# An attention kernel's operand preparation: one copy-and-split pair moved four rounds earlier, a queue wait taken out, and two small schedules shifted

## The chip, the cores and the metric

The kernel runs on one core of one Trainium2 chip. The metric is the device time of one execution in microseconds (us), lower is better. The engines are named PE (TensorE, matrix multiply), DVE (VectorE), ACT (ScalarE), POOL (GpSimd) and SP (SyncE, which here only issues DMAs). PEld is PE's loading of weights.

## What the reference computes

Inputs are x and a context of 4 x 1024 x 512, two gates, and three weight matrices. The first half is a layer norm of x, then attention of 16 heads (32 wide) with the context as keys and values, rotary embedding and a linear bias, and no projections; the second half a feed-forward block with rounded weights and activations.

```python
x = x + tanh(g_xattn[0]) * xattn(layernorm(x), ctx, ctx, 16)
x = x + tanh(g_ffn[0]) * ffn(layernorm(x), w_gate, w_up, w_down)
# xattn: q, k = rope(q), rope(k); softmax(q k^T / sqrt(32) + slope * (j - i)) v
# ffn:   quantized( silu-like(x w_gate^T) * (x w_up^T) ) w_down^T
```

## The kernel before, in words

**Rounds and groups.** Attention goes over 16 groups `p`. A group is one batch and four heads, 128 columns wide. Each group has two halves of queries, and each half eight blocks of keys, so a group has 16 rounds, `w` = 0 to 15 in the code; I call them round 0 to round 15 of group p. A round does on PE four score products (L888), four products for row maxima of the queries three rounds and one half-group ahead (L876), and the product of the previous round's exponentials with the values (L925). ACT takes four exponentials (L1091), of 128 x 512 each. DVE takes two maxima (L1290), of 128 x 1024 each, one for each pair of L876 products. PE's order inside a round is written out by hand: score, score, maximum, maximum, maximum, score, maximum, score, then the values product, then in some rounds a sum of the denominators (L953), a turn of the output (L935) or a turn of a weight tile (L894).

**Two wide banks.** The maxima products land in two PSUM banks of 1024 columns that are used in turn. The order of all uses is a list, and each use waits until the use two places before it has been read out (`bank_release`). The output turns, the weight turns and the "part" uses below stand in the same list. Scores have two banks of their own: score n waits for exponential n - 2.

**Preparing the next groups.** For a later group the queries are normalized by ACT in eight pieces (L1044, `NORM_TILES` tells in which rounds), rotated by POOL in fp32 (`rope`), and split in a high and a low fp16 part in the buffer `S`, in two halves of four blocks. A half takes three steps. ACT writes the high part (`high_part`, L1069). ACT copies the fp32 value to a wide bank (`copy_part`, L1075). DVE subtracts the high part from that copy and writes the low part (`low_part`, L1309). `Step.high` and `Step.low` say in which round each half is split: the query's two halves in rounds 0 and 2 (high) and 1 and 6 (low), the key's in rounds 9 and 12 (high) and 10 and 14 (low). ACT does its high part, then its copy, at the end of a round, after the four exponentials, and DVE does its low part after the round's two maxima. In round 3 or 4 of a group POOL starts a DMA that adds one sum of exponentials onto another (L1822, `Ps<-P`), and again in rounds 6, 11 and 14 or so; the sums go into L953.

**The transposes.** SP sends each half of `S` through a transposing DMA into `QA` or `KA` (`load_stack`, L626). `Step.stack` places these in rounds 0 and 1 (keys), 2 and 9 (queries). SP does not count rounds: it issues in order, each as soon as its waits have been met. The query's second half waits in addition for the accumulation that POOL starts in round 6. The queries' second half is first read in round 13.

**Weights.** The gate weights are prepared beside attention by a table of steps (`gate_weight_jobs`, a step is a round counted over all groups, 16 to a group). At step 85 DVE forms scales (`wscale_r`). At step 89 `wall` brings a maximum to all partitions by DVE instructions alone: one reduction, four transposes and four reductions (L1364 to L1370). `wnorm_1` to `wnorm_3` are three small operations after it.

Of the kernel before, what the change touches and what calls it, by code (L numbers as in the profile page):

```python
# [51 lines left out]
def gate_weight_jobs():  # L52

    jobs = {}

    def put(g, *job):
        jobs.setdefault(g, []).append(job)

    for k in range(OT):
        put(32 + 4 * k, "wload", 0, k)  # L60
        put(38 + 4 * k, "wmax", 0, k)
    put(83, "wscale", 0)
    put(85, "wscale_r", 0)
    put(89, "wall", 0)
    put(94, "wnorm_1", 0)
    put(96, "wnorm_2", 0)
    put(98, "wnorm_3", 0)
    for k in range(OT):
        put(90 + 8 * k, "wload", 0, 12 + k)
        put(100 + 8 * k, "wdivide", 0, k)  # L70
        put(106 + 8 * k, "wround", 0, k)
        put(108 + 8 * k, "wrounded", 0, k)
        put(110 + 8 * k, "wscaled", 0, k)
        put(115 + 8 * k, "wturn", 0, k)
        put(118 + 8 * k, "wstore", 0, k)
    return jobs
# [23 lines left out]

NORM_TILES = {1: (0,), 4: (1, 2, 3), 5: (4,), 6: (5, 6), 7: (7,)}


class Step:


    def __init__(self, g):
        self.g = g  # L110
        self.hf, self.s = hf, s = g // 8, g % 8
        self.p, self.qc = p, qc = hf // 2, hf % 2
        w = 8 * qc + s
        self.inside = 0 <= hf < NHALF
        m = g + 8 + LEAD
        self.hm, self.im = m // 8, m % 8
        self.maxima = 0 <= self.hm < NHALF

        self.out = hf - 1 if s == (3 if hf == NHALF else 4) and 1 <= hf <= NHALF else None


        self.high = self.low = self.key_bias = None
        if -1 <= p and p + 2 < NQ:
            if w == 8:
                self.key_bias = p + 2
            elif w in (9, 12):
                self.high = (p + 2, 1, w // 12)
            elif w in (10, 14):
                self.low = (p + 2, 1, w // 14)
        if 0 <= p and p + 1 < NQ:  # L130
            if w in (0, 2):
                self.high = (p + 1, 0, w // 2)
            if w in (1, 6):
                self.low = (p + 1, 0, w // 6)
        self.side = []

        self.rope = None
        if 0 <= p and p + 2 < NQ and w in (0, 2, 6, 8, 10, 14):
            k = (0, 2, 6, 8, 10, 14).index(w)
            self.rope = (p + 2, 1 - k // 3, k % 3)  # L140
        elif -10 <= g <= -5:
            self.rope = (1, 1 - (g + 10) // 3, (g + 10) % 3)
        self.add = hf - 1 if s == 5 and 1 <= hf < NHALF else None
        self.norm = []
        if 2 <= p + 2 < NQ:
            self.norm += [(p + 2, i) for i in NORM_TILES.get(w, ())]
        if g < -7:
            self.norm += [(1, 2 * (g + 11)), (1, 2 * (g + 11) + 1)] if g < -8 else [(1, 6), (1, 7)]
        self.norm.sort()

        self.load_context = p + 3 if w == 1 and 0 <= p and p + 3 < NQ else None
        self.load_columns = p + 3 if w == 6 and 0 <= p and p + 3 < NQ else None

        self.stack = {0: (1, 0), 1: (1, 1), 2: (0, 0), 9: (0, 1)}.get(w) if 0 <= p and p + 1 < NQ else None
        self.rows = self.hm if 0 <= self.hm < NHALF and self.im == 7 else None
        self.store = p - 1 if w == 7 and 1 <= p <= NQ else None


        last, inside = hf == NHALF - 1, self.inside and hf < NHALF - 1
        self.sum = (hf, s // 2) if last and s % 2 == 1 else (hf, {1: 0, 4: 2, 7: 1}[s]) if inside and s % 3 == 1 else None  # L160
        self.accumulate = (hf, s // 6, s - 1) if inside and s in (3, 6) else None
        self.dens = None
        if s == 6 and inside:
            self.dens = (hf, 0)
        elif s in (1, 2) and 1 <= hf < NHALF:
            self.dens = (hf - 1, s)
        elif last and s in (3, 5, 7):
            self.dens = (hf, s // 2 - 1)
        elif hf == NHALF and s == 1:
            self.dens = (hf - 1, 3)  # L170
        self.num_out = hf - 1 if s == 1 and 1 <= hf <= NHALF else None
        self.den_out = hf - 1 if s == (2 if hf == NHALF else 3) and 1 <= hf <= NHALF else None

        self.stats = None
        if w >= 14 and 0 <= p < NQ:
            self.stats = (p, 0, w - 14)
        elif w == 0 and 1 <= p <= NQ:
            self.stats = (p - 1, 0, 2)
        elif p == NQ and 5 <= w < 8:
            self.stats = (p - 1, 1, w - 5)  # L180
        elif 6 <= w < 9 and 1 <= p < NQ:
            self.stats = (p - 1, 1, w - 6)
        self.aggregate = self.deviation = None
        self.ffn_loads = (hf, s) == (NHALF - 1, 6)


def all_steps():
    steps = [Step(g) for g in range(-8 - LEAD, 8 * NHALF + 8)]
    for jobs in (layer_norm_jobs(), gate_weight_jobs()):
        for st in steps:  # L190
            st.side += jobs.get(st.g, [])
    for i, st in enumerate(steps):
        if 8 * st.qc + st.s == 8 and 1 <= st.p <= NQ and st.p % 4 == 0:
            if st.p < NQ:
                steps[i + 1].aggregate = st.p // 4 - 1
                steps[i + 4].deviation = st.p // 4 - 1
    return steps
# [30 lines left out]
def part_no(p, w, half):  # L228

    return 4 * p + 2 * (1 - w) + half + 1  # L230
# [7 lines left out]
def score_no(hf, kt, h):  # L238
    return 32 * hf + 4 * kt + h + 1
# [352 lines left out]
def sync_program(e, K):  # L592
# [19 lines left out]
    def load_stack(p, w, half):  # L612
        if p >= 2:
            e.wait_ge(K.pe_score, score_no(2 * (p - 2) + 1, 7, 3))
        if w:
            e.wait_ge(K.a_kb, p + 1)
        if p == 0 and half == 0:
            e.wait_ge(K.v_aux, 2)
        if p > 0 and (w, half) == (0, 1):

            e.wait_ge(K.d_acc[1], 16 * (2 * p - 2) + 16)
        e.wait_ge(K.a_hi, part_no(p, w, half))
        e.wait_ge(K.v_lo, part_no(p, w, half))
        rows = slice(4 * half, 4 * half + 4)
        dst = (K.QA, K.KA)[w][p % 2][:, rows, :, :].rearrange("c i h t -> c (i h) t")
        e.dma_start_transpose(dst, K.S[w][:, rows, :, :, :].rearrange("t i h n d -> t (i h n d)")).then_inc(K.d_st[w][half], 16)  # L626
# [63 lines left out]
    for w, half in ((1, 0), (1, 1), (0, 0), (0, 1)):  # L690
        load_stack(0, w, half)
# [3 lines left out]
    for st in STEPS:  # L695
        if st.load_context is not None:
            load_context(st.load_context)
        if st.stack is not None:
            load_stack(st.p + 1, *st.stack)
# [4 lines left out]
        if st.store is not None:  # L704
            p = st.store
# [1207 lines left out]
```

## Time and profile before

| | |
|---|---|
| median of 3 runs | 1842.67 us (1841.62 to 1842.9) |
| the profiled execution's own time | 1842.9 us |
| span in its trace | 1840.9 us |
| PE busy | 1651.6 us, 90% |
| DVE busy | 1486.9 us, 81% |
| ACT busy | 1240.9 us, 67% |
| POOL busy | 814.5 us, 44% |
| mean granted TensorE clock | 0.967 |

The span is from the first to the last instruction; the execution's own time holds about 2 us more. Busy time of PE is a union of records that overlap, so a busy PE is not PE at its peak. Times in views are microseconds from the start of the span, unless they are marked ns. Attention runs from about 62 to 953 us.

### The profile page before, as it was taken

What the parts mean: (1) busy time and instruction counts of PE and PEld (TensorE: products, weight loads), DVE (VectorE), ACT (ScalarE), POOL (GpSimd) and SP (SyncE); (2) the same over time, 40 slices, a digit from 0 to 9 for tenths busy, and PEclk for the clock granted to TensorE, in tenths of its full rate; (3) what the DMA queues carried; (4) which work ended last, traced back from release to release, by engine and by line L of the source; (5) the groups of instructions that cost most, each with busy time, mean ns of one, the idle gap of its engine ahead of it and who ended that gap; (6) DMA issues with size and microseconds to landing.
All of it is one profiled execution on the core that took longest, in us unless ns stands there. A gap on an engine that the chain in (4) does not pass through costs nothing. (4 is left out here: it accounts for less than half of the span.)

```text
span 1840.9 us, 24655 instructions
## 1 busy us (share of the span) xinstructions
PE 1651.6 (90%) x8679; PEld 603.5 (33%) x8679; DVE 1486.9 (81%) x2125; ACT 1240.9 (67%) x1972; POOL 814.5 (44%) x457
## 2 busy tenths in 40 slices
PE   2899999999999999999969999999999910599999
PEld 0222322222322323322213444444444400244444
DVE  6899889998888888888746998868889998855551
ACT  3577888888888888887642332339896699854440
POOL 6489988989999998996620010200000000000000
PEclk9999999999999999999998999999999965799999
DMA  6586878677678786766446898759983469864541
GB/s 170 138 184 156 173 167 181 143 153 156 148 162 170 146 171 142 151 132 138 81 160 168 269 258 254 225 162 277 285 263 134 132 233 285 262 204 167 167 168 66
DMA packets 334202, 331.46 MB, mean 180 GB/s; under 512 B 204640, under 2 KB 263392, under 8 KB 325888
## 3 DMA queue, kind: packets, MB, share of 16 engines
q1 hardware_dynamic: 325152, 264.89, 51.8%
q0 software_dynamic: 8928, 65.02, 17.7%
q8 instruction: 68, 1.11, 0.2%
q14 instruction: 54, 0.44, 0.1%
HBM read 139.92 MB, written 76.55 MB: 118 GB/s over the span
## 5 line engine op out<-in xcount | busy, mean ns | idle before, releaser
L1091 ACT ACTIVATE P<-quad 128x512 f32<-128x512 f32 x1024 | 556.5, 598 | 152.5 <-PE quad L888 149.9
L1290 DVE TENSOR_REDUCE cm<-quad 128x1 f16<-128x1024 f32 x512 | 601.2, 1216 | 71.6 <-PE quad L876 69.2
L1843 POOL TENSOR_TENSOR Ps<-P,P 128x2048 f32<-128x2048 f32 x93 | 424.4, 4564 | 106.3 <-ACT P L1091 106.3
L876 PE MATMUL quad<-KA,QA 100*128 100x512 f16 x1024 | 326.5, 392 | 43.6 <-DMA QA<-S 22.8
L888 PE MATMUL quad<-QA,KA 101*128 101x512 f16 x1024 | 353.7, 386 | 6.7 <-ACT P L1091 5.5
L925 PE MATMUL quad<-P,cg 128*32 128x512 f32 x2048 | 273.6, 606 | 5.2 <-ACT numT L1125 5.2
L968 PE MATMUL quad<-x_hl,Wu 128*128 128x512 f16 x1152 | 249.0, 379 | 2.4 <-DMA Wu<-wt_scratch 2.4
L968 PE MATMUL quad<-x_hl,Wg 128*128 128x512 f16 x1152 | 249.3, 379 | 1.7 <-DMA x_hl<-xs 1.7
L1013 PE MATMUL quad<-Wd,oh 128*128 128x512 f16 x768 | 228.6, 379 | 0.0
L888 PEld LDWEIGHTS quad<-QA,KA 101*128 101x128 f16 x1024 | 83.5, 97 | 331.9 <-ACT P L1091 242.5
L1175 ACT ACTIVATE ev<-quad 128x1024 f32<-128x1024 f32 x96 | 97.2, 1013 | 124.3 <-PE quad L968 118.3
L876 PEld LDWEIGHTS quad<-KA,QA 100*128 100x128 f16 x1024 | 98.6, 99 | 181.9 <-DVE cm L1290 59.1
L968 PEld LDWEIGHTS quad<-x_hl,Wu 128*128 128x128 f16 x1152 | 112.6, 98 | 138.5 <-DMA Wu<-wt_scratch 2.8
L968 PEld LDWEIGHTS quad<-x_hl,Wg 128*128 128x128 f16 x1152 | 112.5, 98 | 138.3 <-issue 3.1
L1551 DVE TENSOR_REDUCE mxt<-ev 128x1 f32<-128x1024 f32 x96 | 116.5, 1214 | 41.5 <-ACT ev L1175 41.2
L1013 PE MATMUL quad<-Wd,ol 128*128 128x512 f16 x384 | 145.5, 379 | 0.0
L1810 POOL TENSOR_TENSOR wq<-wl,wsc 128x512 f32<-128x512 f32 x36 | 41.1, 1141 | 218.3 <-DVE wl L1423 218.3
L1200 ACT ACTIVATE sgm<-gq,qs 128x1024 f32<-128x1024 int16 x96 | 110.1, 1147 | 39.0 <-DVE sgq L1593 37.4
L1689 DVE SCALAR_TENSOR_TENSOR xr<-quad,qs,xr 128x512 f32<-128x512 f32 x32 | 23.9, 750 | 114.6 <-PE quad L1013 110.1
L1013 PEld LDWEIGHTS quad<-Wd,oh 128*128 128x128 f16 x768 | 75.1, 98 | 90.6
L974 PE MATMUL quad<-ident,column 128*128 128x128 f32 x3 | 1.4, 456 | 112.8 <-DVE column L1359 112.8
L953 PE MATMUL quad<-Ps,ones 128*32 128x512 f32 x776 | 101.0, 592 | 1.1 <-POOL Ps L1843 0.8
(163 smaller groups left out, 1945.9 us busy)
## 6 DMA issues: line engine op xcount, KB each, us to landing
Ps<-P POOLq DMA_DIRECT2D x62, 1024.0 KB, 7.6
gate_scratch<-ev SPq DMA_DIRECT2D x48, 512.0 KB, 3.8
gt<-gate_scratch SPq DMA_DIRECT2D x48, 512.0 KB, 5.7
up_scratch<-ev SPq DMA_DIRECT2D x48, 512.0 KB, 3.4
uf<-up_scratch SPq DMA_DIRECT2D x48, 512.0 KB, 4.9
uf<-up_scratch SPq DMA_DIRECT2D x96, 256.0 KB, 3.6
wt_scratch<-wh SPq DMA_DIRECT2D x72, 128.0 KB, 2.3
cg<-in_ctx_dram SPq DMA_DIRECT2D x16, 512.0 KB, 4.7
```

The source lines that it names most:

```text
L876: mm = e.matmul(K.bank(use, c), K.QA[p % 2][0:100, 4 * qc + qt, h, :], K.KA[p % 2][0:100, 4 * c:4 * c + 4, h, :], start=True, stop=True)
L888: e.matmul(K.score[h % 2], K.KA[p % 2][0:101, kt, h, :], K.QA[p % 2][0:101, 4 * qc:4 * qc + 4, h, :], start=True, stop=True).then_inc(K.pe ...
L925: mm = e.matmul(K.num[32 * h:32 * h + 32, :], K.cg[(p + 1) % 4][:, kt, 32 * h:32 * h + 32], K.Pb[before.g % NP][:, h, :], start=kt == 0, s ...
L953: mm = e.matmul(K.den[32 * h:32 * h + 32, :], K.ones[:, :], K.Ps[n % 2 if hf == NHALF - 1 else n][:, h, :], start=n == 0, stop=n == (3 if ...
L968: mm = e.matmul(K.quad[z][:, 512 * h:512 * h + 512], W(part, c), K.x_hl[:, x, c0:c0 + 512], start=n == 0, stop=n == 11)
L1013: mm = e.matmul(ps, o[k][:, ot, sl], K.Wd[r][:, ot, :], start=ot == m == 0, stop=ot == OT - 1 and m == 2)
L1091: e.activation(K.Pb[pb][:, h, :], K.score[h % 2], ACT.Exp, scale=SCALE / (QPOW * KPOW)).then_inc(K.a_exp, 1)
L1175: e.activation(K.ev[k % NEV][:, :], K.quad[k % 4][:, :], ACT.Copy).then_inc(K.a_ev, 1)
L1200: e.activation(K.sgm[n % NSG][:, :], view(n), ACT.Sigmoid, scale=sg).then_inc(K.a_sig, 1)
L1290: e.tensor_reduce(cm[:, col:col + 1], K.quad[UNIT["max", hm, u] % 2][:, :], AX.X, ALU.max).then_inc(K.v_max, 1)
L1551: e.tensor_reduce(K.mxt[:, col:col + 1], K.ev[k % NEV][:, :], AX.X, ALU.max, apply_absolute_value=True).then_inc(K.v_mx, 1)
L1843: e.tensor_tensor(K.Ps[n][:, :, :], K.Pb[(st.g - 1) % NP][:, :, :], K.Pb[st.g % NP][:, :, :], ALU.add).then_inc(K.g_sum, 1)
```

## The change

Four edits. The low part of the second half of the queries goes from round 6 to round 2, behind the high part of the same half. The wait of its transposing DMA on the accumulation is taken out. Tile 0 of the normalization leaves round 1, and the tiles behind it move up by one place: three tiles in rounds 4 and 6, one in 5 and 7. In the weight table `wall` goes two steps earlier (89 to 87) and the three small operations behind it five.

```diff
-    put(89, "wall", 0)
-    put(94, "wnorm_1", 0)
-    put(96, "wnorm_2", 0)
-    put(98, "wnorm_3", 0)
+    put(87, "wall", 0)
+    put(89, "wnorm_1", 0)
+    put(91, "wnorm_2", 0)
+    put(93, "wnorm_3", 0)
...
-NORM_TILES = {1: (0,), 4: (1, 2, 3), 5: (4,), 6: (5, 6), 7: (7,)}
+NORM_TILES = {4: (0, 1, 2), 5: (3,), 6: (4, 5, 6), 7: (7,)}
...
-            if w in (1, 6):
-                self.low = (p + 1, 0, w // 6)
+            if w in (1, 2):
+                self.low = (p + 1, 0, w - 1)
...
-        if p > 0 and (w, half) == (0, 1):
-
-            e.wait_ge(K.d_acc[1], 16 * (2 * p - 2) + 16)
```

## Rows read from the trace of the kernel before

**Rows 1.** The page's first line.

```profile
span 1840.9 us, 24655 instructions
```

**Rows 2.** Windows, groups 1 and 10: length, busy PE, PEld, DVE, ACT, POOL, clock, DMA.

```profile
119.00:177.40 58.40, 54.95 (x321) 15.55 (x321) 57.14 (x88) 45.81 (x86) 53.37 (x41) 1.00 0.75 170
621.30:677.80 56.50, 54.89 (x330) 16.72 (x328) 48.35 (x63) 48.46 (x91) 51.41 (x25) 1.00 0.75 159
```

**Rows 3.** PE in order of time, group 10, start of round 3: start, length, what, count.

```profile
632.10 0.81 PE L876 MATMUL quad<-KA,QA 100*128 100x512 f16 x3
632.75 0.38 PE L888 MATMUL quad<-QA,KA 101*128 101x512 f16 x1
```

**Rows 4.** ACT in order of time, group 10, end of round 2 and start of round 3.

```profile
630.40 1.05 ACT L1069 ACTIVATE S<-t 128x1024 f16<-128x1024 f32 x1
631.35 0.62 ACT L1149 ACTIVATE wi<-wl 128x512 int16<-128x512 f32 x1
632.08 1.08 ACT L1091 ACTIVATE P<-quad 128x512 f32<-128x512 f32 x2
```

**Rows 5.** Group 10: copy and low part of round 1; DVE's next but one pair.

```profile
626.82 0.65 ACT L1075 ACTIVATE quad<-t 128x512 f32<-128x512 f32 x1
...
627.60 0.69 DVE L1309 SCALAR_TENSOR_TENSOR S<-quad,S 128x512 f16<-128x512 f32 x1 [0.37 <-ACT quad L1075]
...
632.73 2.36 DVE L1290 TENSOR_REDUCE cm<-quad 128x1 f16<-128x1024 f32 x2 [1.39 <-PE quad L876]
```

**Rows 6.** Group 10, round 4: DVE reads out a turned weight tile, PE takes the bank.

```profile
635.86 0.69 DVE L1414 TENSOR_TENSOR wh<-quad,wh 128x512 f16<-128x512 f32 x1 [0.77 <-ACT wh L1100]
...
636.61 0.39 PE L876 MATMUL quad<-KA,QA 100*128 100x512 f16 x1 [0.55 <-DVE wh L1414]
```

**Rows 7.** PE in order of time, group 10, round 6.

```profile
642.83 1.06 PE L876 MATMUL quad<-KA,QA 100*128 100x512 f16 x3
```

**Rows 8.** PE in order of time, group 3, round 8.

```profile
260.07 0.96 PE L876 MATMUL quad<-KA,QA 100*128 100x512 f16 x3
```

**Rows 9.** Group 0, end of round 2 and start of round 3: ACT, then PE.

```profile
73.78 1.06 ACT L1069 ACTIVATE S<-t 128x1024 f16<-128x1024 f32 x1
...
74.58 0.81 PE L876 MATMUL quad<-KA,QA 100*128 100x512 f16 x3
75.38 0.39 PE L888 MATMUL quad<-QA,KA 101*128 101x512 f16 x1
```

**Rows 10.** DVE in order of time, group 5, rounds 6 to 10.

```profile
367.08 0.68 DVE L1309 SCALAR_TENSOR_TENSOR S<-quad,S 128x512 f16<-128x512 f32 x1
367.68 0.86 DVE L1497 BATCH_NORM_STATS2 st<-x2s 128x6 f32<-128x128 f32 x4
368.45 2.34 DVE L1290 TENSOR_REDUCE cm<-quad 128x1 f16<-128x1024 f32 x2
...
376.42 0.18 DVE L1364 TENSOR_REDUCE spread<-wmx 128x32 f32<-128x32 f32 x1
...
378.79 2.36 DVE L1290 TENSOR_REDUCE cm<-quad 128x1 f16<-128x1024 f32 x2
```

**Rows 11.** PE, group 5: a score of round 9, the first of round 10, maxima of round 11.

```profile
373.93 0.38 PE L888 MATMUL quad<-QA,KA 101*128 101x512 f16 x1
...
376.82 0.60 PE L888 MATMUL quad<-QA,KA 101*128 101x512 f16 x2
...
381.20 0.98 PE L876 MATMUL quad<-KA,QA 100*128 100x512 f16 x3
```

**Rows 12.** Group 10: POOL's accumulation, SP's transpose, PE's denominators; then L626 over the span.

```profile
644.11 0.89 POOL L1822 DMA_DIRECT2D Ps<-P  x1
...
654.14 2.29 SPq L626 DMA_TRANSPOSE QA<-S  x1
...
658.86 1.04 PE L953 MATMUL quad<-Ps,ones 128*32 128x512 f32 x8
...
DMA to landing us min/median/max: 4.2/5.0/11.6
```

## The prediction

> **What bounds the kernel now.** I first set the span [rows 1] against the execution's own time: the sum below is made against 1842.9 us. The windows by group come next. In group 10 PE is busy 54.89 of 56.50 us, DVE 48.35, ACT 48.46; in group 1 DVE is busy 57.14 of 58.40 [rows 2]. So over most of attention PE sets the pace. In group 1, where the layer norm's statistics still run beside it, DVE does. All four edits lie in attention, and what follows it only starts later or earlier.
>
> Then I read rounds on all engines in order of time. The reader is to see that PE has nearly no slack and that a delay of PE is not made good. Three maxima products come 0.22 us apart, so that three of them last 0.81, the last being 0.38 long, and the third score stands 0.65 behind the first of them [rows 3]. That score also waits for the round's first exponential, which starts at 632.08 and is some 0.6 long, half of the 1.08 of two plus the overlap [rows 4]: it ends at about 632.68, and the score starts at 632.75. So both legs, PE's own queue and scores over exponentials, are tight at once; whatever holds one product inside PE's queue lengthens the round by about as much.
>
> The third maxima product of a round is the sensitive one. It opens the second bank. It waits for the use two places before in the list, which is the second maximum of the round before, or, when a part stands between, that part's DVE read. In group 10's round 6 three products last 1.06 instead of 0.81 [rows 7]: held 0.25 by the maximum. In round 4 the same product waits for a weight tile's read that starts at 635.86 and is 0.69 long, and starts at 636.61, 0.06 behind its end [rows 6]. These are the prices that I use.
>
> **Edit 1, the low part from round 6 to round 2.** Nothing is added or removed: per group one ACT copy (0.65 or 0.61 long) and one DVE subtraction (0.69). It is done for groups 0 to 14, 15 times. What it removes: in the bank list of round 7 the third product now waits for round 6's second maximum, not for the part. The hold of round 6 itself does not go, since it comes ahead of the part and is made by DVE's queue in rounds 4 and 5 (read-out of the output, transposes). In groups 2 to 4, where DVE has a weight maximum of 0.68 in round 6 too, a backlog reaches round 8: three products last 0.96 in place of 0.81 [rows 8], held 0.13 or so. With a DVE operation of 0.6 out of rounds 6 and 7 that goes: 3 x 0.12 = 0.4 gained. From group 6 on there is no such hold to win.
>
> What it adds: the copy now stands behind the high part of the same round. In group 10's round 2 the high part starts at 630.40 and the next ACT operation at 631.35 [rows 4]; that is the place the copy takes, since the code puts it ahead of side work. It ends 0.61 later, at 631.96. DVE started its low part in round 1 at 627.60, 0.13 behind the copy's end at 627.47 [rows 5]; here that gives 632.09, and an end at 632.78 with 0.69. DVE is idle at that time, 1.39 us before its next maximum [rows 5], so its queue does not delay it. PE follows 0.06 later, as in rows 6, at 632.84. The product that waits is the third of round 3, which now starts at 632.10 + 0.43 = 632.53 [rows 3]. Held: 0.31. The last score of the round has a few hundredths of slack, so I take 0.28 for the round. In rounds with side work on ACT the first exponential comes late too (the operation of 0.62 moves back by half a microsecond, of which 0.11 is idle now: 631.97 to 632.08 [rows 4]), about 0.3 to 0.4, and by the same amount beside the first, not on top. The bounds of this term: nothing, if the copy were done by ACT ahead of the high part, which the code excludes, so 0.2 from the scatter of the three handovers; above, 0.4 from ACT's leg.
>
> The same for groups 2 to 14: 13 x 0.28 = 3.6 us. Group 0's round 2 has no denominators on PE, so less room: the high part starts at 73.78, the next ACT operation at 74.73, the copy there would end at 75.34, the low part run from 75.47 to 76.16, and the third product start at 76.22 in place of 74.58 + 0.43 = 75.01. The third score then starts at 76.44 in place of 75.38 [rows 9]: 1.06 us. I take off 0.1 for group 0's own backlog in round 8: 0.95. In group 1 DVE has 1.26 us of idle in all [rows 2]; the operation that goes out of round 6 comes in in round 2, ahead of all of its later waits: 0, between -0.6 and +0.6.
>
> **Edit 2, the weight maximum in round 7 of group 5, in place of round 9.** It is a row of nine DVE operations, from 376.42 until the next maximum at 378.79: 2.37 us [rows 10]. DVE works without a pause there since round 5 has the scale operations too. Rounds 7 and 8 are short ones, without denominators; rounds 9 and 10 are long, and DVE catches up in them, which is why the maximum costs little now: a hold of 0.17 of the three products in round 11 (0.98 long) and a late start of about 0.2 [rows 11], 0.33 together. After the change: DVE's low part is out (367.08 to 367.68, 0.60), so round 7's pair starts at 367.85 in place of 368.45. The pair takes 2.26 (2.34 less an overlap of 0.08), the nine operations run from 370.11 to 372.48, a reduction takes 0.6, and round 8's pair starts at 373.08; its second maximum starts 1.13 later and ends at 375.43. Round 9's third product waits for that: 375.49, and the score behind it at 375.71, in place of 373.93 [rows 11]. From that score to the first of round 10 it is 2.89 now (376.82 less 373.93), of which some 0.24 is a wait for ACT that the delay covers. So 375.71 + 2.65 = 378.36 in place of 376.82: 1.54 later; less 0.33 for round 11, 1.2 us. This holds the first edit's gain in group 5. Bounds: 0, if DVE's row went into idle time, to 2.4, its whole length. The three small operations behind it move into rounds 9, 11 and 13: below 0.1.
>
> **Edit 3, normalization tiles.** Round 1 loses an ACT operation behind which ACT is idle, round 4 keeps three, round 6 gets a third where the copy went. Round 7's stays, so that POOL's rotation in round 8 is not earlier. Zero; it is hidden in ACT's idle time.
>
> **Edit 4, the wait of the transposing DMA.** SP issues it at 654.14, when the accumulation issued at 644.11 has landed [rows 12]: 10.0 us. Without the wait it goes behind the store of the same group, some seven us earlier. Nothing waits for it before round 13, so nothing is gained. What is queued behind it on SP (a weight tile, the row of round 12) is not waited for either. What it may cost is the accumulation itself: PE needs it at 658.86, 14.75 behind its issue [rows 12], so 4.7 us of slack. A transpose lands in 5.0 at the median [rows 12]. If its whole time were added to the accumulation's 10.0, it would land 0.3 late. So zero, up to 0.3 for each of 14 groups.
>
> A page of the Trainium skill speaks on this, and against the change: "DMA: Bandwidth & Descriptors", section "Queues, rings and completion order", says that each DMA engine goes round between its queues packet by packet. By that rule POOL's accumulation and SP's transpose share the engines while both are in flight, and the landing would move back. By rule the sum would be up to 4 us higher than mine; the rows of this trace, where the two are kept apart in round 6, don't show it.
>
> **Sum.** 0.95 + 3.6 - 0.4 + 1.2 = 5.4, of which I round off to 5.3: 1842.9 + 5.3 = 1848.2 us. The median of the runs shown is 0.2 under the profiled execution, so against it the forecast is 1848.0.
>
> **Rivals.**
> (a) The copy is not what PE waits for, or the delay is made good. Speaks for it: 0.3 us is three handovers of 0.06 to 0.13, each of which I carry over from another round. Against it: both legs are tight in rows 3 and 4. Then 0.95 and 1.2 at most remain, less 0.4: 1843 to 1845, no change to be told. It decides at a low part that ends by 632.47.
> (b) The transpose collides with the accumulation, and the denominators' product of round 10 waits. Price: at a transpose of 5.0 us 0.3 per group, 14 groups: +4, so 1852. With the longest, 11.6 [rows 12], 6.9 per group, about +95; I give that no weight. Against it: the store and weight transfers ahead of the transpose on SP's queue keep it back anyway. It decides at a landing more than 14.7 us after the issue.
> (c) Faster: if the hold in rows 7 is made by the copy and the part in round 6 after all, the change takes 0.25 from each of 15 groups, 0.4 from rows 8 and group 5's part, and round 3 hides the copy: -3.8 to -4.5, 1838.7. It decides where DVE's pair in round 6 starts. Against it: the part comes after the held product.
> (d) Edit 4 does nothing, since SP is held otherwise at that time: no change to the sum.
>
> **Chances.** Forecast 0.62; (b) 0.08, also slower; (a) 0.22; (c) 0.08. What a measurement of this kernel tells from no change is about 0.2%, 3.7 us: below 1839.0 it is faster, above 1846.4 slower. The forecast's own range reaches from 13 x 0.2 and half of edit 2 (+3.5) to 13 x 0.4 and all of it (+8.5), so a part of it, 0.05, lies within 0.2%. Slower 0.65, the same 0.27, faster 0.08. The range takes in most of (a), not (c): 1843.0 to 1852.0.
>
> **What would show it.** Right: in rounds 3 of groups 2 to 14 the three maxima products last about 1.1 us and not 0.81, with a wait for L1309; group 5 has PE wait for DVE in round 9 by well over 1 us; groups 6 to 14 are each 0.28 longer; L626 is issued before the accumulation lands, and L953 does not wait for it. Wrong: no wait in round 3; a wait of L953 for the accumulation in round 10 (b); three products in round 6 at 0.81 (c). The prediction fails most easily by the 0.28, which counts 13 times.

## The result, and the profile after

The changed kernel takes 1865.22 us in the median of four runs (1858.28 to 1875.63), the kernel before 1842.14 (1841.43 to 1842.9, four runs); the ratio is 1.013, with a 95% interval of 1.0082 to 1.0179. The forecast was 1848.2 us with a range up to 1852.0: the direction was right, the size was not.

The profiled execution of the changed kernel took 1867.81 us. Its page begins with the first line below, against [rows 1]; the second is from the page's groups (busy, mean ns of one, idle before it and what ended that idle time), and tells where to look: PE idled 17.6 us for `Ps` ahead of the denominators, which are L950 here. All later lines of the code stand three lower than in the trace of before.

```profile
span 1865.9 us, 24641 instructions
...
L950 PE MATMUL quad<-Ps,ones 128*32 128x512 f32 x776 | 102.3, 599 | 18.7 <-DMA Ps<-P 17.6
```

To find the place, take the time from one round's first exponential to the next round's as the length of the round. From the first exponential to the end of the last it is 914.87 us, and 891.07 before: 23.8 of the 25.0 us of span lie in attention. By group: 19.61 in group 1, 3.08 in group 5, 0.15 to 0.31 in each of groups 2 to 4 and 6 to 14 (3.1 together), none in 15, and -2.02 in group 0. Group 1 has 18.87 of it in round 10, 22.61 us long in place of 3.74, and 0.83 in round 11.

**Group 1.** These are SP, POOL and PE in order of time (start, length, then the instruction, with idle time and its releaser in brackets).

```profile
142.84 1.78 SPq L609 DMA_DIRECT2D xl<-in_x_dram  x1
144.77 8.30 SPq L623 DMA_TRANSPOSE QA<-S  x1
...
140.85 0.20 POOL L1742 TENSOR_TENSOR nwt<-mv,eps 128x8 f32<-128x8 f32 x1
...
144.84 0.20 POOL L1742 TENSOR_TENSOR nm<-nwt,minus 128x8 f32<-128x8 f32 x1
145.32 0.92 POOL L1819 DMA_DIRECT2D Ps<-P  x1 [0.28 <-ACT P L1088]
...
156.55 1.06 PE L922 MATMUL quad<-P,cg 128*32 128x512 f32 x8
175.19 1.94 PE L950 MATMUL quad<-Ps,ones 128*32 128x512 f32 x8 [17.57 <-DMA Ps<-P]
```

The reader is to see the order. POOL does ten small operations of the layer norm from 140.85 to 145.04, and only then issues the accumulation, at 145.32. SP, which no longer waits for it, has issued the transpose at 144.77, 0.55 ahead. The accumulation lands at 175.15, 29.8 us after its issue, and PE starts 0.04 later. Three loads and a store that SP issued from 140.91 to 142.84 stand ahead of the transpose; all four are still in flight at 145.32, and the last lands at 150.3. In all other groups the accumulation is issued first, and there it hardly suffers: in groups 2 to 14 it lands 8.5 to 11.1 us after its issue (7.8 to 10.8 before), and it is the transpose that takes longer, 9.7 to 14.0 (4.3 to 6.0 before). This is group 10, where nothing is late (compare [rows 12]):

```profile
666.76 0.89 POOL L1819 DMA_DIRECT2D Ps<-P  x1
...
670.41 8.08 SPq L623 DMA_TRANSPOSE QA<-S  x1
...
681.51 1.04 PE L950 MATMUL quad<-Ps,ones 128*32 128x512 f32 x8
```

and the shortest, median and longest landing times of L623 and, behind it, of L1819 over the span:

```profile
DMA to landing us min/median/max: 4.3/5.9/28.5
...
DMA to landing us min/median/max: 6.9/7.5/29.8
```

The view of the DMA queues shows that both transfers slow down together (a packet is a piece of a transfer that one of the 16 DMA engines carries). It is that of 146 to 175 us after, in which POOL's next accumulation, issued at 162.04, has begun too (q0 is POOL's queue, q1 SP's; the share is that of 16 engines' time):

```profile
DMA packets 3207, 2.73 MB, mean 94 GB/s; under 512 B 2139, under 2 KB 2877, under 8 KB 3020
...
q0 software_dynamic: 208, 1.52, 67.3%
q1 hardware_dynamic: 2998, 1.20, 50.5%
```

and the same for 147 to 161 us of the kernel before, which holds its accumulation and its transpose:

```profile
DMA packets 3316, 2.34 MB, mean 167 GB/s; under 512 B 2134, under 2 KB 3044, under 8 KB 3187
...
q1 hardware_dynamic: 3171, 1.28, 36.7%
q0 software_dynamic: 144, 1.05, 36.1%
```

A packet of POOL's took 0.673 x 16 x 29 / 208 = 1.50 us, against 0.361 x 16 x 14 / 144 = 0.56; one of SP's 78 ns against 26, by the same working. These are means, and the single packets in the trace tell more. The median packet lasts as long as before, 0.63 us on POOL's queue and 18 ns on SP's. But 34 of POOL's 208 last over 0.7 us, up to 13.8, and hold 69% of the queue's packet time, where before none of 144 did; on SP's queue 172 of 2998 last over 0.12 us and hold 70%, where before none did. At each full microsecond of the stall 14 to 28 packets are in flight. So the engines were not idle, but for most of the time they sat on a few very long packets, and moved 94 GB/s in place of 167.

Behind the stall PE is slow too: its clock falls at 162.3, after PE has waited since 157.6. The windows (length, busy PE, PEld, DVE, ACT, POOL, granted clock, DMA) show the clock near the lower of its two levels, 1.2 GHz, until 179.5; the eight denominator products at 175.19 last 1.94 and not 1.04. That is the rest of the 18.9 us, and the 0.83 of round 11.

```profile
157.00:175.00 18.00, 0.62 (x8) 0.00 (x0) 2.86 (x5) 0.86 (x2) 6.21 (x4) 0.65 0.91 79
175.00:179.50 4.50, 4.31 (x15) 1.12 (x16) 0.52 (x1) 1.57 (x3) 0.00 (x0) 0.52 0.61 127
```

**Group 10** is as forecast. ACT, DVE and PE around the start of round 3, against [rows 3 to 5]:

```profile
652.75 1.05 ACT L1066 ACTIVATE S<-t 128x1024 f16<-128x1024 f32 x1
653.70 0.60 ACT L1072 ACTIVATE quad<-t 128x512 f32<-128x512 f32 x1
654.22 0.62 ACT L1146 ACTIVATE wi<-wl 128x512 int16<-128x512 f32 x1
...
654.43 0.69 DVE L1306 SCALAR_TENSOR_TENSOR S<-quad,S 128x512 f16<-128x512 f32 x1 [0.73 <-ACT quad L1072]
...
654.45 1.12 PE L873 MATMUL quad<-KA,QA 100*128 100x512 f16 x3
655.40 0.38 PE L885 MATMUL quad<-QA,KA 101*128 101x512 f16 x1
```

The window of the whole group, against [rows 2]:

```profile
643.70:700.50 56.80, 55.05 (x330) 16.74 (x329) 48.41 (x63) 48.35 (x92) 51.41 (x25) 1.00 0.75 158
```

The copy stands behind the high part, the low part ends at 655.12, and PE's third product comes after it: three products last 1.12, not 0.81. The third score is 0.95 behind the first product, not 0.65.

**Group 5.** PE in order of time, and then the window of the same stretch.

```profile
390.60 0.60 PE L885 MATMUL quad<-QA,KA 101*128 101x512 f16 x2
392.73 0.60 PE L873 MATMUL quad<-KA,QA 100*128 100x512 f16 x2 [1.53 <-DVE cm L1287]
393.86 0.39 PE L873 MATMUL quad<-KA,QA 100*128 100x512 f16 x1 [0.53 <-DVE cm L1287]
...
395.24 1.94 PE L922 MATMUL quad<-P,cg 128*32 128x512 f32 x8
396.94 1.45 PE L950 MATMUL quad<-Ps,ones 128*32 128x512 f32 x8
```

```profile
392.90:397.00 4.10, 3.57 (x18) 0.77 (x20) 3.76 (x4) 2.23 (x4) 2.32 (x2) 0.68 0.52 121
```

PE waits for DVE twice, and right behind that eight products of the output last 1.94, where they lasted 1.06 before the wait (L922 in group 1, above), at a mean granted clock of 0.68.

**Group 0.** PE's hold is there: the third product of round 3, against [rows 9]. Round 3 is 0.48 longer than before. Why the group as a whole is 2.0 shorter is told below, under "Group 0".

```profile
71.61 0.60 PE L873 MATMUL quad<-KA,QA 100*128 100x512 f16 x2
73.24 0.39 PE L873 MATMUL quad<-KA,QA 100*128 100x512 f16 x1 [1.03 <-DVE S L1306]
```

### The profile page after: what moved, and what is told of

It is laid out like the page before. It is cut to its first block and busy times, and to the rows that moved or that the text cites. A ratio compares the mean times of both kernels' runs of the same rounds, so it can differ in the third digit from the quotient of the medians.

```text
span 1865.9 us, 24641 instructions
## 1 busy us (share of the span) xinstructions
PE 1654.3 (89%) x8679; PEld 602.7 (32%) x8679; DVE 1488.6 (80%) x2125; ACT 1239.7 (66%) x1972; POOL 815.1 (44%) x457
## 3 DMA queue, kind: packets, MB, share of 16 engines
q8 instruction: 68, 1.11, 0.2%
## 5 line engine op out<-in xcount | busy, mean ns | idle before, releaser
L922 PE MATMUL quad<-P,cg 128*32 128x512 f32 x2048 | 273.6, 606 | 5.2 <-ACT numT L1122 5.2
L950 PE MATMUL quad<-Ps,ones 128*32 128x512 f32 x776 | 102.3, 599 | 18.7 <-DMA Ps<-P 17.6
```

What stands on the lines that cost most here:

```text
L922: mm = e.matmul(K.num[32 * h:32 * h + 32, :], K.cg[(p + 1) % 4][:, kt, 32 * h:32 * h + 32], K.Pb[before.g % NP][:, h, :], start=kt == 0, s ...
L950: mm = e.matmul(K.den[32 * h:32 * h + 32, :], K.ones[:, :], K.Ps[n % 2 if hf == NHALF - 1 else n][:, h, :], start=n == 0, stop=n == (3 if ...
```

## The experiments

All times are medians beside runs of the kernel before on the same chip: 1842.93 us for the first four kernels, 1842.97 for the next four, 1842.78 for the last three. On these chips single runs scatter more than in the first comparison (before: 1837.34 to 1862.44; e1, with the wait in place, has one run of 1871.37, e4 one of 2027.04), so small effects are read from the traces. Two parts of a trace differ without any edit: group 0 (see below), and what follows attention, which lasts 888.0 us in the trace of before, 888.9 to 890.9 in ten others, but 893.2 in that of e5 and 895.3 in that of e3. Groups 3 to 15 of two traces agree to 0.02 where nothing was edited and nothing stalls.

| kernel | edit | us | ratio [95% interval] | round 10 of group 1 |
|---|---|---|---|---|
| e1 | after, wait back | 1850.18 | 1.0048 [1.0028, 1.0068] | 3.75 |
| e2 | before, wait gone | 1847.44 | 1.0016 [0.9994, 1.0038] | 16.78 |
| e3 | after, wait in group 1 alone | 1849.11 | 1.0037 [1.0022, 1.0051] | 3.74 |
| e4 | before, low part moved | 1846.36 | 1.0017 [1.0006, 1.0028] | 3.75 |
| e5 | before, `wall` moved | 1846.62 | 1.0024 [0.9999, 1.0050] | 3.74 |
| e6 | after, accumulation first | 1849.67 | 1.0033 [1.0011, 1.0055] | 3.74 |
| e7 | after, transpose early | 1849.39 (one) | - | 3.74 |
| e8 | before, row turns later | 1840.91 | 0.9982 [0.9960, 1.0005] | 3.74 |
| e9 | after, accumulation later | 1936.48 | 1.042 [1.0401, 1.0440] | 3.74 |
| e10 | before, two edits | 1837.45 | 0.9972 [0.9962, 0.9982] | 3.74 |
| e11 | after, unaltered | 1870.17 | 1.0104 [1.0040, 1.0168] | 20.49 |

### The wait: e1, e2, e3

e1 puts the wait back into the changed kernel; e2 takes only it out of the kernel before; e3 has it in the changed kernel for one transpose, that of group 1:

```diff
+        if p == 2 and (w, half) == (0, 1):
+
+            e.wait_ge(K.d_acc[1], 16 * (2 * p - 2) + 16)
```

> The changed kernel with the wait of the query's second transpose on the accumulation put back; the other three edits stay. Theory C (collision): the 18.9 us that round 10 of group 1 lasts too long come from the transpose and the accumulation being in flight together, so they go, and the time is that of my forecast without them, 1848 to 1849 us (ratio 1.003), with round 10 of group 1 at 3.7 us, and little scatter. Rival W (the bank order or the early low part by itself delays the accumulation or the denominators in group 1): the time stays near 1865.

> The kernel before with only the wait taken out; the low part stays in round 6. In group 1 the low part ends at 146.3 us, so SP can issue the transpose at about 146.4, some 0.4 us ahead of the accumulation's issue at 146.84. Theory C (both in flight is enough, with the transpose ahead of the accumulation): a stall of 10 us or more in round 10 of group 1, 1852 to 1870. Rival O (the low part in round 2 is needed, since only then the transpose is well ahead): no stall, 1842.5. In all other groups the transpose is issued well behind the accumulation, and no denominators wait.

> The changed kernel with the wait put back for the one transpose that is issued in group 1, none for the 13 others. Theory C with one place: as the run with the wait everywhere, 1848 to 1849. Rival (the collision moves to the next group, or costs a little in each): between 1850 and 1865, with a wait of L950 for the accumulation in another group.

With the wait back, all of the stall goes; one wait, in group 1, is enough. With only the wait taken out of the kernel before, the profiled run (1856.82 us) shows the stall too. The rows are e2's SP, POOL and PE:

```profile
145.13 4.95 SPq L623 DMA_TRANSPOSE QA<-S  x1
...
145.54 0.91 POOL L1819 DMA_DIRECT2D Ps<-P  x1 [0.28 <-ACT P L1088]
...
170.09 1.94 PE L950 MATMUL quad<-Ps,ones 128*32 128x512 f32 x8 [11.74 <-DMA Ps<-P]
```

PE's idle time there is 11.74 us, not 17.57. e2's median of 1847.44 misses my 1852 to 1870, and its ratio of 1.0016 is not told from no change. Its ten runs reach from 1840.34 to 1869.78, which suggests that the stall differs from one execution to the next; only one of them has a trace, so this isn't shown. Taken together, e1 and e3, each with the changed kernel's stall gone, show that the wait's removal makes the 19 us, in one place.

### The order: e6, e7, e9, e11

e6 moves the layer norm's small operations by one step, so that POOL issues the accumulation of group 1 first:

```diff
-            jobs.setdefault(n - 2, []).append(("deviation", n // 8))
+            jobs.setdefault(n - 1, []).append(("deviation", n // 8))
```

> The changed kernel, the wait still out, with POOL's ten small operations of the layer norm one step later, so that the accumulation in group 1 is issued by 142.5 us, ahead of the transpose at 144.8, as it is in all other groups. Theory order (the stall comes when the accumulation starts behind a transpose that is in flight): no stall, 1848 to 1850, the accumulation lands in 9 to 12 us. Rival overlap (any time in which both are in flight in group 1, with the row loads in front of them, does it): a stall of 10 us or more stays, 1858 or more.

```profile
146.34 9.90 SPq L623 DMA_TRANSPOSE QA<-S  x1
...
142.38 0.85 POOL L1819 DMA_DIRECT2D Ps<-P  x1
```

Without any wait, and with the accumulation 3.96 us ahead, the stall is gone: they land after 10.9 and 11.9 us.

e7 puts the transpose ahead in every group, in round 6:

```diff
-        self.stack = {0: (1, 0), 1: (1, 1), 2: (0, 0), 9: (0, 1)}.get(w) if ...
+        self.stack = {0: (1, 0), 1: (1, 1), 2: (0, 0), 6: (0, 1)}.get(w) if ...
...
+        if p > 1 and (w, half) == (0, 1):
+            e.wait_ge(K.g_x2, 2 * p - 2)
```

> The changed kernel with the query's second transpose issued in round 6 in front of the load of x, as soon as POOL's addition is done, so at about the time of the accumulation's issue in every group from 1 on; its packets then run for some 4 us and the accumulation's start in the middle of them. Theory order: a stall in nearly every group, 10 to 20 us each, 2000 us or more. Rival (group 1 is special: its queue holds three row loads and a store ahead of the transpose): a stall in group 1 at most, under 1870.

That was wrong: 1849.39 us, the time of e1. In most groups the transpose got out about 0.1 us behind the accumulation, not ahead. In group 1 it was ahead by 4.4 us, in group 0 by 1.45, and the accumulations landed after 9.6 and 10.1. Once, in group 13 with the transpose 0.11 behind, the accumulation took 15.0 us and held PE by 0.27:

```profile
816.96 0.85 POOL L1821 DMA_DIRECT2D Ps<-P  x1
...
817.07 12.41 SPq L625 DMA_TRANSPOSE QA<-S  x1
```

So a transpose ahead, or in flight, is not enough. But e7 changed more than the order: its transpose also stands ahead of the load of x and the store that are in front of it in the other kernels. e9 has POOL issue the accumulation behind its rotary work of the step, 2.3 us later:

```diff
+        if st.rope is not None:
+            rope(*st.rope)
         if st.accumulate is not None:
...
-        if st.rope is not None:
-            rope(*st.rope)
```

> The changed kernel, with the DMA that adds the two halves of P issued by GpSimd behind that step's rotary work and not ahead of it, so about 2.3 us later; in groups 4, 5, 6, 13 and 14 the transpose is then ahead of it by an estimated 0.4 to 1.7 us, in groups 2, 3 and 7 to 12 it is not. My theory (a transpose that is in flight when the accumulation's transfer starts slows both): in those five groups the accumulation lands well over 12 us after its issue, in one or more of them TensorE waits for Ps at the denominators of round 10, and the kernel takes 1850 to 1900 us, varying from one execution to the next; the other groups keep 9.4 to 11 us. Rival (group 1 stalls for what is special there, its row loads and other transfers of that stretch, and not for the order): the accumulations of the five groups land after 9.4 to 11 us as before, and the time is that of the changed kernel, group 1's stall and nothing else.

It took 1916.16 to 1950.73 us, more than the 1850 to 1900 that I expected (1.051 by the medians; the interval in the table is that of its two shortest runs). A line of its page, and then group 6 as an example:

```profile
L950 PE MATMUL quad<-Ps,ones 128*32 128x512 f32 x776 | 105.5, 616 | 90.5 <-DMA Ps<-P 89.7
```

```profile
477.54 14.41 SPq L623 DMA_TRANSPOSE QA<-S  x1
...
478.65 0.87 POOL L1821 DMA_DIRECT2D Ps<-P  x1
...
509.94 1.93 PE L950 MATMUL quad<-Ps,ones 128*32 128x512 f32 x8 [18.63 <-DMA Ps<-P]
```

Round 10 is 24.76, 25.08, 14.86 and 23.67 us long in groups 0, 4, 5 and 6. The transposes there are ahead by 0.74, 0.51, 1.09 and 1.11. Groups 13 (ahead by 1.75) and 14 (behind by 0.60) have no stall, and group 1, now ahead by 1.77, has none either. A fifth stall is in round 2 of group 9 (26.54), where the accumulation of round 15 of group 8 and the transpose of the keys were issued 0.06 apart. My theory was right in its kind and wrong in its list: of the five groups named three stalled, and of the others two. The rival, that group 1 is special, has fallen.

e11 is the changed kernel again.

> The changed kernel once more, unaltered, for a second execution of it with a profile. My theory (the transpose is issued ahead of the accumulation in round 6 of group 1, both transfers slow down together, by an amount that varies): TensorE waits for Ps in round 10 of group 1 by 5 to 20 us and in no other group, and the time is 1855 to 1875 us. Rival (the first profile showed a chance event that has nothing to do with the order): no such wait, about 1849 us, or one in another group.

```profile
143.67 8.98 SPq L623 DMA_TRANSPOSE QA<-S  x1
...
145.17 0.91 POOL L1819 DMA_DIRECT2D Ps<-P  x1 [0.28 <-ACT P L1088]
...
172.95 1.93 PE L950 MATMUL quad<-Ps,ones 128*32 128x512 f32 x8 [15.45 <-DMA Ps<-P]
```

The same stall, with the transpose 1.50 ahead. Its runs took 1848.2 to 1883.73 us; the first of these has room for no stall.

All thirteen traces together, in pairs of an accumulation and a transpose issued within 12 us of each other: of 11 in which the transpose is 0.3 to 1.6 us ahead, seven accumulations landed 24 to 33 us after their issue. Of 56 in which it is 1.6 to 4 us ahead none took over 9.2, though a transpose alone takes 4.3 or more and so these are in flight together for a while as well. Of 16 that are up to 0.3 ahead one collapsed (32.3), and of 37 up to 1 us behind the one of e7 took 15.0.

The delay isn't all that sets these pairs apart. In all seven that collapsed, two to four of SP's other transfers, issued ahead of the transpose, were still in flight when the accumulation was issued, and the last of them landed 3.5 to 5.1 us later. Of the four that did not, two had none in flight, and in the other two (group 0 of e7, round 3 of group 1 of e9) the last landed 1.2 and 0.9 later. Of the 56 pairs only one had more than one in flight, the last landing 2.6 later. Company alone isn't enough either: e9 has five pairs with the transpose 0.07 to 0.11 ahead and four such transfers in flight, and they landed after 9.1 to 11.0; and the one at 0.06 that collapsed had none. No experiment varied this by itself, so the range of 0.3 to 1.6 us is that of these pairs and no rule.

### The other edits: e4, e5

e4 is the kernel before with the low part alone moved, e5 that with the four `put` lines of the diff alone.

> The kernel before with the low part in round 2 and nothing else changed. My forecast's first term: 0.26 to 0.31 per group in groups 2 to 14, less 0.4, and group 1 about even. In the changed kernel group 0 did not become longer but 2.0 shorter, so group 0 is taken from there: -2.0 to 0. Sum: +1.5 to +4, 1844 to 1846.5. Rival (the low part costs nothing by itself, the tiles of the normalization do): 1840 to 1842.

> The kernel before with only the weight maximum and its three small operations moved. The low part stays in round 6 of group 5. In the changed kernel group 5's round 9 grew by 3.7 us: 2.1 are holds of PE by DVE, and after them the granted clock is at its lower level for 3.4 us. Theory (DVE's backlog in the two short rounds, then the clock): +3 to +5, with a stretch of granted clock 0.5 in round 9 or 8 of group 5, 1846 to 1848. Rival (my forecast's term, holds alone): +1.2 to +2, no stretch at the lower clock.

e4: groups 7 to 12 are 0.30 longer, 6, 13 and 14 0.25, 2 to 4 0.15, group 5 0.34 shorter. e5: group 5 is 57.87 us long in place of 56.09 and groups 1 to 4 and 6 to 15 are as before; group 0 is 1.43 shorter. What follows attention is 5.3 us longer in this trace, which this edit doesn't touch, so e5's time is no measure of the edit. PE's holds are 1.53 and 0.53, as in the changed kernel, but the clock stays up behind them. In the traces of after, e1, e3, e6 and e7 it falls, and group 5 takes 59.15 to 59.17. Here are e1's window and, behind it, e5's:

```profile
375.50:379.40 3.90, 3.90 (x20) 0.63 (x18) 2.20 (x2) 2.23 (x4) 2.54 (x1) 0.56 0.42 99
```

```profile
375.00:382.00 7.00, 7.00 (x47) 1.95 (x46) 5.31 (x6) 5.22 (x10) 5.63 (x2) 1.00 0.15 41
```

So the rival of e5 was right of this run: 1.8 us by the holds alone. e11, with both edits, had no fall either (57.52), nor did group 5 of e9 have one behind its two holds. The fall is worth 59.17 - 57.52 = 1.65 where it comes.

### A version that beats both: e8, e10

The prediction puts the hold of rounds 6 and 14 down to DVE's queue. e8 takes the turning of the row maxima out of that round and does it one later (`turn_rows(late_rows)` in place of `turn_rows(st.rows)`).

> Not a part of the change: the kernel before with DVE's four transposes of the row maxima (0.89 us) one round later, behind the maxima of rounds 5 and 13. It tests the step of my forecast that says the hold of round 6 and 14 is made by DVE's queue in rounds 4 and 5 and not by the low part. Theory: the hold of 0.22 goes from rounds 6 and 14 of nearly all groups, -0.21 x 28 = -6 us, 1836 to 1838. Rival (the low part or the statistics make it): it stays and the time is 1842 to 1844.

Rounds 6 and 14 are 3.74 in place of 3.95 from group 6 on, so the queue makes that hold; but groups 2 to 4 lose 0.3 each and group 5 1.7, part of it by a fall of the clock from 367.4 to 370.9. So the time is 1840.91, not told from no change, and not my 1836 to 1838. e10 keeps it for groups 6 to 14 alone and moves group 5's scaling later:

```diff
-    put(85, "wscale_r", 0)
-    put(89, "wall", 0)
-    put(94, "wnorm_1", 0)
-    put(96, "wnorm_2", 0)
-    put(98, "wnorm_3", 0)
+    put(89, "wscale_r", 0)
+    put(97, "wall", 0)
+    put(101, "wnorm_1", 0)
+    put(102, "wnorm_2", 0)
+    put(104, "wnorm_3", 0)
...
-        if st.rows is not None:
-            turn_rows(st.rows)
+        if late_rows is not None:
+            turn_rows(late_rows)
+        late_rows = None
+        if st.rows is not None and st.rows < 12:
+            turn_rows(st.rows)
+        elif st.rows is not None:
+            late_rows = st.rows
```

> The kernel before, with VectorE's row sums (the transposition of the row factors) one round later in groups 6 to 14 alone, which took 0.21 us off rounds 6 and 14 each and cost groups 2 to 5 more in rounds 0 and 8; and with the weight scaling of group 5 and its norms put at steps 89, 97, 101, 102 and 104, where TensorE has more ahead of it. Theory: 9 groups by 0.41 is 3.7 us less, and up to 1.7 us less in group 5, so about 1837.5 us, ratio 0.997. Rival (what group 5's scaling delays is only put elsewhere, and the late sums cost in round 0 and 8 of the other groups too): 1841 to 1844 us.

1837.45 us, 5.3 less than before. Groups 7 to 14 are 0.40 shorter each, and group 5 takes 54.12 in place of 56.09; what the scaling costs instead, 0.43 in round 3 of group 6, eats that group's own gain. PE in order of time, round 6 of group 10, against [rows 7], and that round 3, which stands ahead of it:

```profile
404.67 0.39 PE L876 MATMUL quad<-KA,QA 100*128 100x512 f16 x1 [0.30 <-DVE cm L1290]
...
636.95 0.81 PE L876 MATMUL quad<-KA,QA 100*128 100x512 f16 x3
```

## Why the prediction was wrong

**The step that failed** is edit 4: "So zero, up to 0.3 for each of 14 groups", and with it the price of rival (b). I gave the mechanism, a landing more than 14.7 us after the issue, and a chance of 0.08, but priced it as the sum of two undisturbed landing times. Measured: nothing in 13 groups, and 18.9 us in one (29.8 us to the landing, and the clock behind it). A sum of the two, as rival (b) has it, would be 9.5 + 4.3 = 13.8 us by the rows of group 1 before, within PE's 14.7; where the accumulation went first it didn't even grow by that. Two things were missing. First, the order: I assumed that the store and the weight tiles keep the transpose back in every group. I looked at group 10, where POOL has nothing else to do; in group 1 it has ten small operations ahead of the issue, and [rows 2] already told that this group is not like the others. Second, I had set aside the large end of the bounds ("about +95; I give that no weight"). e9 shows a loss of that size, 94 us, from the same two transfers.

The Trainium skill's "DMA: Bandwidth & Descriptors", section "Queues, rings and completion order", says that an engine alternates between its queues packet by packet. By that rule both transfers would share the engines and land some us later. e6 agrees with that (10.9 and 11.9 where they take 9.5 and 4.3 apart). The stall is beyond it: one after the other the two take 13.8 us, and here the accumulation took 29.8, with single packets of up to 13.8 us, so it isn't the sharing alone.

**Right.** The 0.28 of round 3: measured 0.26 in groups 2 to 4, 6, 13 and 14, and 0.30 in groups 7 to 12, there by way of the late exponential, which I had named beside it. The low part's handover, forecast at 0.13 behind the copy, and PE's third product behind it are in the rows. The gain in round 8 of groups 2 to 4: 0.11 each, forecast 0.12. Edit 3 at nothing: e4, which has the old tiles, and e1 have the same groups to 0.01 but for group 5. Group 1 even with the wait back (58.42 against 58.38). The groups 1 to 15 of e1 are 6.1 us longer than before. Forecast for them were 3.6 - 0.4 + 1.2 = 4.4, and 1.65 of the rest is the clock's fall in group 5. That e1's profiled run, 1848.79 us, comes so near to the 1848.2 of the forecast is luck in part: group 0 is 1.4 shorter in it, where 0.95 longer was forecast, since its clock came up earlier (see below); what follows attention is 1.3 longer by nothing that the edits do; and the clock's fall was not in the forecast. Its median is 1850.18, 7.3 more than before.

**Mis-sized.** Group 5. Forecast were 1.2 for edit 2 and 0.28 for edit 1, together 1.5, and e11, with both and no fall of the clock, has 1.43. (e5's 1.78 is edit 2 without the low part's move, which by e4 gives 0.34 there.) Where the clock falls behind the holds, as in the changed kernel, the group is 3.1 longer. The step "which is 2.89 now ... So 375.71 + 2.65" took PE's speed behind a wait for granted; 1.65 us of clock are missing from it.

**Group 0.** Its hold was forecast at 1.06 and is there, at 1.03, but the group is 2.0 shorter than before. In the six us from 66 to 72 PE does 19 products in the trace of before and 31 after. The windows of before and, behind it, of after:

```profile
66.00:72.00 6.00, 6.00 (x19) 1.47 (x18) 3.14 (x3) 4.34 (x9) 2.55 (x1) 1.00 0.00 1
```

```profile
66.00:72.00 6.00, 5.65 (x31) 1.37 (x31) 5.23 (x5) 5.56 (x11) 4.10 (x1) 1.00 0.51 49
```

The granted clock of 1.00 misleads here. The trace's record of the clock begins with a step to the full clock, at 72.1 us in the trace of before and at 63.3 after; ahead of that step there is no record, and the view counts what it has no record of as 1.00. The products themselves tell it. These are PE's of before on either side of 72.1:

```profile
67.25 0.63 PE L888 MATMUL quad<-QA,KA 101*128 101x512 f16 x1
...
72.39 0.38 PE L888 MATMUL quad<-QA,KA 101*128 101x512 f16 x1
```

So the difference is in the main the time at which the clock came up, and the change didn't make it: e5, e2 and e10 are the kernel before throughout group 0, have the step at 68.9, 69.5 and 63.8, and take 55.73, 55.96 and 54.52 us for it, against 57.16. Kernels with the low part in round 2 compare with these at a like step: e6, at 69.3, takes 56.78, so 0.8 to 1.05 more, and after, at 63.3, takes 55.14, so 0.6 more than e10. My 0.95 lies in that.

**Open.** Why the two transfers collapse when the transpose is issued 0.3 to 1.6 us ahead and hardly ever otherwise, and whether SP's other transfers in flight, which go with the seven collapses of 11, are a part of the cause. The issue of the accumulation lasts 0.9 us, and its first packet starts 1.9 us behind the issue in group 1 before, 5.0 after; what meets what in that time no view shows. Nor was it tried whether a smaller or a plain transfer in the transpose's place does the same.

## What to carry to other kernels

A wait whose result nobody needs may be all that fixes the order of two transfers. Before taking one out, list the issue times of both in every repetition, above all in those where the issuing engine has extra work, and not in a typical one. Then keep the order by the engines' own programs (e6 does it without a wait, at no cost to be seen: 1849.67 us against e1's 1850.18) or keep the wait, which costs nothing where nobody waits for its transfer, as here. And a hold of an engine is not only its length: add what the clock may take behind it. When two executions of the same code differ near the start, look at when the clock came up before you put it down to an edit.

## What was unexpected of the hardware

- A DMA transpose issued 0.3 to 1.6 us ahead of an accumulating DMA of 1 MB can make both take 24 to 39 us, where they take 4.3 and 9.5 apart; in all seven cases two to four other transfers of SP's were in flight too. Most packets last as ever then, and a few last up to 13.8 us. PE's idle time for it was 17.57 and 15.45 us in the two traces of the changed kernel; the times of e11 (1848.2 to 1883.73 us) suggest that it can also stay away.
- The granted clock fell behind holds as short as 1.53 and 0.53 us: to 0.56 over the next 3.9 us in e1; after the same holds in the changed kernel eight products took 1.94 in place of 1.06. Behind the same holds it stayed at 1.00 in e5 and e11.
- At the start of attention the clock came up at 63.1 to 72.1 us of the span in the thirteen traces, and with the same code group 0 took 54.52 us (step at 63.8) to 57.16 (at 72.1).
